# One attention iteration of a decoder layer, its steps in another order on all five engines, and one semaphore for a second set of weights

## The reference

```python
def attn(x):                                     # x after layernorm
    scores = einsum('bqe,bke->bqk', x @ W_qk, x) * SCALE + (kpos - qpos) * slope
    p = softmax(where(causal, scores, -inf))
    return einsum('bqk,bkd->bqd', p, x @ W_v.T)
def xattn(Q, ctx, mask):                         # Q after layernorm, 16 heads
    q, k, v = heads(Q @ wq.T), heads(ctx @ wk.T), heads(ctx @ wv.T)
    p = softmax(where(mask, -inf, einsum('bhqd,bhkd->bhqk', q, k) / sqrt(16)))
    return merge(einsum('bhqk,bhkd->bhqd', p, v)) @ wfc.T
def ffn(x):                                      # x after layernorm
    topk_vals, topk_idx = top_k(softmax(x @ w_gate), 2)
    gate = normalised(topk_vals placed at topk_idx)
    g, u = split(einsum('bsd,edh->ebsh', x, w_gate_up))
    return einsum('bse,ebsd->bsd', gate, einsum('ebsf,efd->ebsd', silu(g) * u, w_down))
x = x + attn(ln(x));  x = x + xattn(ln(x), ctx, mask);  x = x + ffn(ln(x))
```

## Time and profile before

| what | value |
|---|---|
| median of 3 runs | 1101.05 us (1100.43 to 1101.15) |
| the profiled execution | 1097.28 us, its span 1095.5 us |
| iterations 1 to 13 of the attention loop | 89.97 to about 459.9 us of the span |
| PE busy | 1026.1 us, 94% |
| ACT, DVE, POOL busy | 644.5, 648.0, 519.5 us |
| DMA | 160.84 MB, mean 147 GB/s |
| mean granted TensorE clock | 0.987 |

### The profile page before, as it was taken

How to read it: one execution, slowest core, us unless ns; L and a number is a source line. 1 busy time by engine, 2 the same in 40 slices (tenths; PEclk the granted TensorE clock), 3 DMA queues, 4 the chain that set the end, 5 groups by cost and what they waited for, 6 DMA issues and landing times.

```text
span 1095.5 us, 36805 instructions
## 1 busy us (share of the span) xinstructions
PE 1026.1 (94%) x12856; PEld 863.5 (79%) x12856; DVE 648.0 (59%) x2144; ACT 644.5 (59%) x1410; POOL 519.5 (47%) x564
## 2 busy tenths in 40 slices
PE   4689999999999999978989999999999999999994
PEld 2456677767677666646988999999999999999984
DVE  5566777777777787874565444444444444444442
ACT  5678888888888888854443344343343343443431
POOL 4755677777777777523334323223223333223223
PEclk9989999999999999999999999999999999999998
DMA  5654667766666555359122543742635442215761
GB/s 179 208 191 154 179 184 183 183 183 169 174 172 182 168 178 159 100 196 345 41 31 36 150 116 77 248 144 53 199 75 162 135 144 34 34 29 149 299 217 16
DMA packets 92929, 160.84 MB, mean 147 GB/s; under 512 B 21184, under 2 KB 69376, under 8 KB 88000
## 3 DMA queue, kind: packets, MB, share of 16 engines
q1 hardware_dynamic: 77598, 141.83, 40.4%
q0 software_dynamic: 15248, 18.18, 9.8%
q10 hardware_dynamic: 18, 0.01, 0.0%
HBM read 270.75 MB, written 43.07 MB: 286 GB/s over the span
## 4 chain that ended last, share of the span: by engine, by line
PE 81%; DMA 4%; DVE 4%; SPq 4%; ACT 3%; issue 2%; POOL 1%; another core or an unknown queue 0%; ACTq 0%; DVEq 0%; POOLq 0%
PE t_ring L2461 15%; PE front L2461 15%; PE pv L2493 7%; PE s_ring L2493 7%; PE pv L2164 6%; PE s_ring L2131 5%; PE t_ring L2149 4%; PE front L2006 3%; PE front L2015 3%; DMA q_stack<-q_lo 2%; PE front L2064 2%; PE tail L2015 2%; PE s_ring L1993 2%; PE tail L1993 1%; PE tail L2209 1%
## 5 line engine op out<-in xcount | busy, mean ns | idle before, releaser
L881 POOL DMA_INDIRECT out<-y_sb,place_i x64 | 101.8, 1591 | 287.5 <-DVE y_sb L1901 92.7
L1377 DVE TENSOR_REDUCE nmax<-s_ring 128x2 f32<-128x512 f32 x256 | 167.3, 681 | 59.7 <-PE s_ring L2131 57.1
L2461 PE MATMUL t_ring<-rows_hi,wgu_sb 128*128 128x128 f16 x2048 | 193.9, 220 | 1.1 <-issue 1.1
L2461 PE MATMUL front<-rows_hi,wgu_sb 128*128 128x128 f16 x2048 | 192.4, 219 | 1.6 <-DVE rows_lo L1874 1.6
L1048 ACT ACTIVATE probs_t<-t_ring,mask_bias 128x512 f32<-128x512 f32 x256 | 167.1, 701 | 27.4 <-PE t_ring L2149 25.0
L2461 PE MATMUL t_ring<-rows_lo,wgu_sb 128*128 128x128 f16 x1024 | 179.3, 220 | 0.0
L2461 PE MATMUL front<-rows_lo,wgu_sb 128*128 128x128 f16 x1024 | 178.1, 219 | 0.0
L2461 PEld LDWEIGHTS front<-rows_hi,wgu_sb 128*128 128x128 f16 x2048 | 162.7, 98 | 3.9 <-DVE rows_lo L1874 2.1
L2461 PEld LDWEIGHTS t_ring<-rows_hi,wgu_sb 128*128 128x128 f16 x2048 | 163.6, 98 | 2.2 <-issue 0.6
L1238 ACT ACTIVATE silu_g<-t_ring 128x256 f32<-128x256 f32 x136 | 52.3, 384 | 164.0 <-PE t_ring L2461 148.1
L1238 ACT ACTIVATE silu_g<-front 128x256 f32<-128x256 f32 x136 | 52.0, 383 | 161.2 <-PE front L2461 143.9
(11 more groups left out here) (324 smaller groups left out, 2269.1 us busy)
## 6 DMA issues: line engine op xcount, KB each, us to landing
wgu_sb<-gu_split SPq DMA_DIRECT2D x68, 2048.0 KB
wd_sb<-down_split SPq DMA_DIRECT2D x68, 1024.0 KB
w_piece<-in_w_gu SPq DMA_DIRECT2D x32, 512.0 KB
gu_split<-w_halves SPq DMA_DIRECT2D x32, 512.0 KB, 3.8
w_piece<-in_w_down SPq DMA_DIRECT2D x16, 512.0 KB
down_split<-w_halves SPq DMA_DIRECT2D x16, 512.0 KB, 5.1
x_in<-in_x SPq DMA_DIRECT2D x16, 256.0 KB, 3.6
ctx_in<-in_ctx_t_in SPq DMA_DIRECT2D x16, 256.0 KB
```

What stands on the lines that cost most here:

```text
L881: nc.gpsimd.indirect_dma_start(out=out, out_offset=bass.IndirectOffsetOnAxis(ap=place_i[:, j:j + 1], axis=0), in_=y_sb[:, j], in_offset=No ...
L1377: nc.vector.tensor_reduce(nmax[:, n // HJ, :, n % HJ], s_ring[n % 2][:].rearrange("p (r k) -> p r k", r=2), AX.X, ALU.max, negate=True).th ...
L2461: o = nc.tensor.matmul(gu_ring[f][:, part * SLOT:(part + 1) * SLOT], wgu_sb[j][:, w, at:at + P], r[:, j % 2, c], start=(i == 0), stop=(i = ...
```

## The change

The calls inside `iteration` are put into another order on SP, GpSimd, ScalarE, VectorE and TensorE. No call is added or removed, and no wait inside the moved calls is changed. The iterations 14 and 15, the start and the second phase keep their orders. Beside that, the two sets of semaphores `wgu_b_in` and `wd_b_in` become one, `second_in`: the wait for a second set's down weights is made together with the one for its gate and up weights, before the mixed slot's first matmul.

```diff
-        wgu_b_in, wd_b_in = sems("wgu_b_in", 3), sems("wd_b_in", 3)
+        second_in = sems("second_in", 3)
...
@@ SP, iteration @@
+                if f and (not isinstance(b, int) or b + 4 < B):
+                    load_next(b + 4, p)
+                if f:
+                    store_pieces(b + 2, h + 1, p)
+                if c:
+                    store_stream(b - 1)
                 if n:
                     load_pieces(b + 3, h + 1 + p, 1 - p)
-                if f and (not isinstance(b, int) or b + 4 < B):
-                    load_next(b + 4, p)
-                if f:
-                    store_pieces(b + 2, h + 1, p)
-                    stack_rows(b + 2, p)
-                    stack_k_hi(b + 2, p)
                 if s and f:
                     stack_max(b + 1, 1 - p)
                 if f:
-                    stack_k_lo(b + 2, p)
+                    stack_rows(b + 2, p)
                     stack_q_hi(b + 2, p)
                     stack_q_lo(b + 2, p)
+                    stack_k_hi(b + 2, p)
+                    stack_k_lo(b + 2, p)
                 if c:
                     store_normed(b - 1, 1 - p)
-                    store_stream(b - 1)
...
@@ TensorE, iteration, up to the first h_scores and at the end @@
+                if f:
+                    f_xnt(b + 2)
                 if c:
                     t_half(b - 1, q, 0, s_ring[0])
-                if f:
-                    f_xnt(b + 2)
-                if c:
-                    t_half(b - 1, q, 1, s_ring[1])
-                if f:
-                    f_k(b + 2)
                 if t:
                     pe.wait_ge(max_stacked[p], 16 * h + 16)
                     h_scores_t(b, p, 0, 0)
...
                 if c:
-                    t_ont(b - 1)
-                if f:
-                    f_k_rest(b + 2)
+                    t_half(b - 1, q, 1, s_ring[1])
                 if t:
                     h_scores_t(b, p, 1, 0)
+                    h_scores_t(b, p, 1, 1)
                 if f:
                     f_q1_rest(b + 2)
-                if t:
-                    h_scores_t(b, p, 1, 1)
+                    f_k(b + 2)
                 if c:
-                    t_fc(b - 1)
+                    t_ont(b - 1)
                 if s:
                     h_scores(b + 1, q, h + p, 0, 2)
-                if c:
-                    t_fc_rest(b - 1)
                 if f:
                     f_scores(b + 2)
+                    f_k_rest(b + 2)
...
                 if f:
                     f_v2(b + 2)
-                    f_q(b + 2)
                 if s:
                     h_max(b + 1)
-                if f:
+                if t:
+                    h_values(b, p, 7)
+                if f:
+                    f_q(b + 2)
                     f_q_rest(b + 2)
...
@@ TensorE, mixed slots @@
-                    pe.wait_ge(wgu_b_in[second_of(s - FULL)], 16 * ((s - FULL) // 3) + 16)
+                    pe.wait_ge(second_in[second_of(s - FULL)], 32 * ((s - FULL) // 3) + 32)
...
-                if mixed and f == 0:
-                    pe.wait_ge(wd_b_in[second_of(s - FULL)], 16 * ((s - FULL) // 3) + 16)
```

More of the change, by code:

```diff
@@ L790, in iteration @@
                     scatter_first(b - 2, p, h + p - 1)
+                if f:
+                    ctx_rest(b + 2)
+                if parted:
+                    scatter_part(p, 1)
                 if c:
@@ L2264, in iteration @@
                     h_values(b, p, 0)
+                    h_values(b, p, 1)
+                    h_scores_t(b, p, 2, 0)
+                    h_scores_t(b, p, 2, 1)
+                if s:
+                    h_scores(b + 1, q, h + p, 4, 5)
+                    h_scores(b + 1, q, h + p, 5, 6)
+                if c:
+                    t_fc(b - 1)
+                    t_fc_rest(b - 1)
                 if f:
@@ L2267, in iteration @@
                 if s:
-                    h_scores(b + 1, q, h + p, 4, 5)
-                if t:
-                    h_scores_t(b, p, 2, 1)
+                    h_scores(b + 1, q, h + p, 6, 7)
                 if f:
                     f_probs_t(b + 2)
-                if s:
-                    h_scores(b + 1, q, h + p, 5, 6)
-                if t:
-                    h_values(b, p, 1)
-                if s:
-                    h_scores(b + 1, q, h + p, 6, 7)
                 if t:
@@ L2283, in iteration @@
                     h_scores(b + 1, q, h + p, 7, 8)
+                    h_scores(b + 1, q, h + p, 8, 9)
                 if f:
@@ L2286, in iteration @@
                 if s:
-                    h_scores(b + 1, q, h + p, 8, 9)
+                    h_scores(b + 1, q, h + p, 9, 10)
                 if t:
@@ L2290, in iteration @@
                     h_scores_t(b, p, 4, 1)
-                    h_values(b, p, 2)
+                if s:
+                    h_scores(b + 1, q, h + p, 10, 11)
                 if c:
@@ L2294, in iteration @@
                 if t:
+                    h_values(b, p, 2)
                     h_values(b, p, 3)
-                if s:
-                    h_scores(b + 1, q, h + p, 9, 10)
+                if c:
+                    t_gate(b - 1)
                 if t:
@@ L2300, in iteration @@
                 if s:
-                    h_scores(b + 1, q, h + p, 10, 11)
+                    h_scores(b + 1, q, h + p, 11, 12)
                 if t:
@@ L2306, in iteration @@
                 if s:
-                    h_scores(b + 1, q, h + p, 11, 12)
-                if c:
-                    t_gate(b - 1)
+                    h_scores(b + 1, q, h + p, 12, 14)
                 if t:
@@ L2312, in iteration @@
                     h_values(b, p, 5)
-                    h_scores_t(b, p, 7, 0)
-                if s:
-                    h_scores(b + 1, q, h + p, 12, 14)
-                if t:
-                    h_scores_t(b, p, 7, 1)
                 if f:
@@ L2320, in iteration @@
                 if t:
-                    h_values(b, p, 6)
+                    h_scores_t(b, p, 7, 0)
                 if s:
@@ L2324, in iteration @@
                 if t:
-                    h_values(b, p, 7)
+                    h_scores_t(b, p, 7, 1)
+                    h_values(b, p, 6)
                 if s:
```

111 lines of the change are left out of this document (52 added, 59 removed).

## The result

The changed kernel takes **1184.79 us** (median of 4 runs, 1180.97 to 1188.46); the kernel before, on the same chip, 1100.74 (4 runs, 1099.24 to 1101.15). The ratio is 1.0761, with a 95% interval from 1.0735 to 1.0787: slower by 84 us. The profiled execution has a span of 1182.2 us against 1095.5.

The account below looks back on a forecast made before the run. The prediction took TensorE (94% busy) as the bound, with SP's queue ending each period almost together with it. 13 x (3.2 + 0.1) + 3.3 = 46 plus 13 x 1.3 = 17 gave +63: 1164 us, range 1141 to 1190.

Parts of the forecast that it names:

- S: Start of `h_scores(0, 2)` on TensorE in the attention loop; SP's queue alone was to put it 11.6 us after `f_v2` ends.

Follow-up runs that it names:

- the 32 matmuls: Changed kernel plus 32 matmuls on constant data, result unread, on TensorE ahead of the wait for the maxima in each iteration; 1167.01 us, ratio 1.0600.
- the late load: Changed kernel with load_pieces moved back to first in SP's iteration, stack transfers kept in the new order; 1169.53 us, ratio 1.0688.
- the stack order: Changed kernel with stack_rows and k_hi put back ahead of the wait for the maxima, load_pieces kept late; 1201.48 us, ratio 1.0951.
- the small pieces: Changed kernel, iterations 1 to 10 loading only 64 of each piece's 1024 columns, same instructions and queue order; 1173.59 us, ratio 1.0702.

## What to carry to other kernels

When TensorE is made to wait some microseconds in every iteration, add to the wait the half clock behind it, in full: no placing of the wait hid it here, it only moved it from one side of S to the other. Only work put into the wait (the 32 matmuls) won part of it back. When two edits lengthen waits on the same engine, price them as one list of events and not as a sum: undoing one alone (the late load) brought back 8 us of 84, undoing the other (the stack order) cost 21 more. And for each moved instruction ask which queue waits for it to release a buffer, not only who reads its result.

## What the runs showed of the hardware

- From the issue of 8 KB to the start of the engine that waits for it: 2.1 us with the small pieces, 7.2 (median) behind 3 MB of stores and loads in its own queue, 6.4 beside them from another engine's queue.
- SP needed 2.83 us to issue three loads of 512 KB right behind the stores, 2.81 for three of 32 KB at the same place (with the small pieces), and 1.42 for the three of 512 KB in the kernel before, right behind `store_normed` and `store_stream` (323.39 to 324.81). The DMA share was 1.0 or more in all three places. So neither the size of the loads nor the share sets this; what does stays open.
- In the stretches shown of the changed kernel and of the one with small pieces, the granted clock fell to 0.50 during the wait and stayed there for 4.5 to 5.1 us after TensorE's work began again, where the slow stretch of the earlier trace rows lasted 3.1 us. It can also fall after the wait: with the maxima on ScalarE's queue TensorE began again at 329.20, after 2.40 us idle, with matmuls of 0.61 in a row of four; the window from 329 to 330 has a clock of 1.00 and the one from 330 to 331 has 0.53.
- Small transfers can fill the engines too: in the version with small pieces the DMA share was up to 1.01 at 128 GB/s while hardly anything but the stacks passed, in rows of 1 KB (512 elements of two bytes):

```profile
329.00:330.00 1.00, 0.53 (x5) 0.28 (x3) 0.00 (x0) 1.00 (x3) 0.84 (x2) 1.00 1.01 128
```
